# An eight-head masked attention layer: the work in front of the first attention row, reordered

## What is computed

```python
h = jnp.maximum(_layernorm(x, axis=-1), 0.0)
q = (h @ Wq + bq).reshape(b, n, H, HD)
k = (h @ Wk + bk).reshape(b, n, H, HD)
v = (h @ Wv + bv).reshape(b, n, H, HD)
scores = jnp.einsum('bqhd,bkhd->bhqk', q, k) / jnp.sqrt(jnp.float32(HD))
scores = scores + (1.0 - adj)[None, None, :, :] * -1000000000.0
attn = jax.nn.softmax(scores, axis=-1)
out = jnp.einsum('bhqk,bkhd->bqhd', attn, v).reshape(b, n, d)
return x + (out @ Wo + bo)
```

## Time and profile before

| | us |
|---|---|
| median of 3 runs | 1139.5 (1138.93 to 1139.97) |
| profiled execution, its own time | 1138.54 |
| span of the profiled execution | 1136.6 |
| PE busy | 1101.3 (97%) |
| ACT busy | 1019.7 (90%) |
| DVE busy | 964.0 (85%) |
| POOL busy | 131.5 (12%) |

### The profile page before, as it was taken

One profiled execution on the slowest core, in us unless ns is written; L12 is line 12 of the kernel. 1 busy time (PEld: TensorE's weight loads), 2 busy tenths in 40 slices (PEclk: granted clock), 3 DMA queues, 4 the chain that ended last, 5 costly groups with the idle time before them and its releaser, 6 DMA issues.

```text
span 1136.6 us, 28159 instructions
## 1 busy us (share of the span) xinstructions
PE 1101.3 (97%) x10756; PEld 894.8 (79%) x10756; DVE 964.0 (85%) x1747; ACT 1019.7 (90%) x1883; POOL 131.5 (12%) x234
## 2 busy tenths in 40 slices
PE   5599999999999999999999999999999999999997
PEld 4378888888878878888887878878887887878775
DVE  4599889988899888998889978898889988888875
ACT  2499999999999999999999999999999999999995
POOL 3102000021000210021001200012000021000001
PEclk9699999999999999999999999999999999999999
DMA  8532242423423243332423324242242323223101
GB/s 276 154 94 58 60 125 64 106 59 79 127 62 94 55 120 93 76 93 56 124 75 86 94 57 129 60 105 73 71 124 59 103 57 97 72 73 90 45 20 38
DMA packets 76596, 99.51 MB, mean 88 GB/s; under 512 B 17968, under 2 KB 43696, under 8 KB 76464
## 3 DMA queue, kind: packets, MB, share of 16 engines
q1 hardware_dynamic: 75504, 95.10, 31.6%
q0 software_dynamic: 576, 1.57, 0.6%
q10 hardware_dynamic: 384, 1.05, 0.3%
...
## 4 chain that ended last, share of the span: by engine, by line
PE 90%; ACT 6%; DVE 1%; ACTq 1%; issue 1%; DMA 1%; POOL 0%; DVEq 0%
PE ps_turn L693 29%; PE ps_scores L679 22%; PE ps_heads L756 18%; PE ps_side L700 9%; PE ps_side L727 5%; PE ps_side L709 5%; ACT rows L439 3%; ACT turned_a L444 1%; ACTq L278 1%; PE ps_turn L700 1%; PE ps_heads L716 1%; PE ps_heads L742 1%; ACT turned_b L449 0%; DMA xn<-in_x 0%; DVE rows L529 0%
## 5 line engine op out<-in xcount | busy, mean ns | idle before, releaser
L529 DVE CUSTOM_DVE_ANT_0 rows<-ps_scores,mask 128x1024 f32<-128x1024 f32 x512 | 613.0, 1215 | 32.0 <-issue 23.7
L439 ACT ACTIVATE rows<-rows,row_min 128x1024 f32<-128x1024 f32 x512 | 587.2, 1150 | 17.7 <-DVE row_min L529 17.4
L693 PE MATMUL ps_turn<-ident_r,rows_raw 128*128 128x128 f32 x4096 | 462.9, 256 | 6.6 <-ACT turned_a L444 4.9
L693 PEld LDWEIGHTS ps_turn<-ident_r,rows_raw 128*128 128x128 f32 x4096 | 399.0, 141 | 74.0 <-issue 35.5
L444 ACT ACTIVATE turned_a<-ps_turn 128x512 f32<-128x512 f32 x512 | 305.5, 597 | 52.1 <-PE ps_turn L693 52.0
L679 PE MATMUL ps_scores<-k_stack,q_stack 128*128 128x512 f32 x1024 | 317.5, 422 | 12.8 <-DMA k_stack<-start_k_lo 12.1
L536 DVE COPY turned_b<-ps_turn 128x512 f32<-128x512 f32 x328 | 225.6, 688 | 35.8 <-PE ps_turn L693 27.1
L679 PEld LDWEIGHTS ps_scores<-k_stack,q_stack 128*128 128x128 f32 x1024 | 167.1, 189 | 35.8 <-issue 14.8
L417 POOL COPY inv_wide<-row_inv 128x256 f32<-128x256 f32 x64 | 25.5, 399 | 943.9 <-DVE row_inv L564 916.1
L756 PE MATMUL ps_heads<-turned_a,v 128*32 128x256 f32 x2048 | 123.8, 382 | 0.6 <-ACT inv_wide L474 0.6
L756 PE MATMUL ps_heads<-turned_b,v 128*32 128x256 f32 x2048 | 122.2, 379 | 0.0
...
## 6 DMA issues: line engine op xcount, KB each, us to landing
q_stack<-q_hi SPq DMA_DIRECT2D x240, 64.0 KB, 2.0
q_stack<-q_lo SPq DMA_DIRECT2D x240, 64.0 KB, 2.0
k_stack<-k_hi SPq DMA_DIRECT2D x240, 64.0 KB, 2.0
k_stack<-k_lo SPq DMA_DIRECT2D x240, 64.0 KB, 2.0
...
```

What stands on the lines that cost most here:

```text
L439: nc.scalar.activation(rows[:, k, :], rows[:, k, :], ACT.Exp, bias=row_min[:, k:k + 1], scale=-1.0, accum_out=row_sum[:, u % 2, j:j + 1]). ...
L529: nc.vector.tensor_tensor_reduce(out=rows[:, k, :], in0=ps_scores[n % 2][:], in1=mask[:, qt, :], scale=1.0, scalar=START_MIN, op0=ALU.add, ...
L693: tr = nc.tensor.transpose(ps_turn[half][:, k, :].bitcast(F32R), rows_raw[:, n % RING, kt * P:(kt + 1) * P], ident_r[:])
```

## The change

- PE runs 20 matmuls of the identity (128x512, WARM) before its first real work.
- START_STEPS is reordered: q's first half, k's first half, then the second "ht" pair, k's second half, q's second half. Counts that followed s now follow the place in START_QK. The start tiles are 512 wide; the second halves use the steady tiles `q_hi`, `k_hi`, `q_lo`, `k_lo`.
- The stack copies of the start are made by halves, in DMAs of 64 KB: q's first half (16) by POOL; k's first half (16) by SP; k's second half by ACT for heads 0 and 1 (8), by POOL for head 2 (4), by SP for head 3 (4). q's second half (16) is issued by SP after the fourth row's scores. So 48 DMAs of 64 KB (3 MB) stand ahead of row 3, where 32 of 128 KB (4 MB) stood.
- x of batch 0 is loaded in three pieces; the first two hold two tiles each.
- Mask tile 1 is loaded early and converted by DVE between the low parts. Tiles 2 and 3 and tiles 4 to 7 are loaded by SP after the fourth row's scores and converted by POOL, tile by tile (`late_masks`). The load of x for batch 1 and the first two of the residual stand behind them.
- In batch 0 no moments of batch 1 are taken before row 8; those of tiles 0 to 3 all follow row 8.
- ACT's high part of q for phase 1 now waits for all 16 copies of q's second half out of `q_hi` (`stack_count` gives 4 DMAs per head for it, 1 before).

```diff
-START_STEPS = (("ht", 0), ("ht", 1), ("qk", 0), ("ht", 2), ("ht", 3), ("qk", 1), ("qk", 2), ("qk", 3),
+START_STEPS = (("ht", 0), ("ht", 1), ("qk", 0), ("qk", 1), ("ht", 2), ("ht", 3), ("qk", 3), ("qk", 2),
                ("v", 0), ("v", 1))
+START_QK = [s for kind, s in START_STEPS if kind == "qk"]
+WARM = 20
+MASKS_EARLY, MASKS_LATE = 2, 4
...
             count = (fills * CHUNKS + steps_more) * STEP_DMAS
             if g == 0:
-                first = PARTS - POOL_COPIES if n == "q" else 0 if h < ACT_HEADS else PARTS
-                count += first - CHUNKS * STEP_DMAS
+                count -= STEP_DMAS if n == "q" else CHUNKS * STEP_DMAS
...
+            sp.wait_ge(lo_done, START_QK.index(1) + 1)
+            stack_step(sp, 0, 1, start_stacked, high=start_hi, low=start_lo)
+            sp.wait_ge(lo_done, START_QK.index(3) + 1)
+            stack_step(sp, 0, 3, start_stacked, range(ACT_HEADS + 1, PARTS))
+
+            sp.wait_ge(scores_done, PARTS)
+            load_mask(2, MASKS_EARLY, MASKS_LATE)
+            stack_step(sp, 0, 2, stacked["q"][0])
+            load_mask(3, MASKS_LATE, TILES)
+            load_x(1)
             load_res(0, 0)
             load_res(0, 1)
...
-            pool.wait_ge(lo_done, QK_STEPS - 1)
-            for h in range(PARTS):
-                stack_start(pool, pool_stacked[h], h, "q", range(POOL_COPIES))
+            pool.wait_ge(lo_done, START_QK.index(0) + 1)
+            stack_step(pool, 0, 0, pool_stacked, high=start_hi, low=start_lo)
+            pool.wait_ge(lo_done, START_QK.index(3) + 1)
+            stack_step(pool, 0, 3, pool_stacked, range(ACT_HEADS, ACT_HEADS + 1))
...
+            def late_masks(part, first, end):
+                pool.wait_ge(mask_in[part], 16)
+                for t in range(first, end):
+                    pool.tensor_scalar(mask[:, t, :], mask[:, t, :], 1.0, -MASKED, ALU.subtract, ALU.mult
+                                       ).then_inc(mask_ready, 1)
+
+            late_masks(2, MASKS_EARLY, MASKS_LATE)
...
-            act.wait_ge(lo_done, QK_STEPS)
-            for h in range(ACT_HEADS):
-                stack_start(act, act_stacked[h], h, "k", range(PARTS))
+            act.wait_ge(lo_done, START_QK.index(3) + 1)
+            stack_step(act, 0, 3, start_stacked, range(ACT_HEADS))
...
-            for s in range(QK_STEPS):
-                cols = slice(s // 2 * BANK, (s // 2 + 1) * BANK)
-                low_part(0, 0, s, start_lo[s % 2][:, cols], start_hi[s % 2][:, cols], QK_BANKS[s % 2])
+            for k, s in enumerate(START_QK):
+                low_part(k + 1, 0, s, (start_lo + lo)[s][:], (start_hi + hi)[s][:], QK_BANKS[k % 2])
...
-                    if g == 0 and STATS[t] == i and not last:
+                    if g == 0 and i == max(STATS[t], 0 if b else UNIT_ROWS) and not last:
                         moments(b + 1, t)
...
+            for _ in range(WARM):
+                nc.tensor.matmul(ps_scores[1][:, 0:BANK].rearrange("p (k n) -> p k n", n=P), ident_r[:],
+                                 ident_r[:].unsqueeze(1).to_broadcast([P, PARTS, P]), start=True, stop=True)
```

105 lines of the change are left out of this document (53 added, 52 removed).

## The result

The changed kernel takes 1133.33 us (median of 5 runs, 1132.61 to 1133.84) where the kernel before takes 1139.48 (5 runs, 1138.93 to 1139.97): a ratio of 0.9946, with a 95% interval from 0.9932 to 0.9961. The medians are 6.15 us apart, the two profiled executions 5.05 (1138.54 and 1133.49; spans 1136.6 and 1131.3).

A forecast was written before the change was run, and what follows sets the result against it. The prediction took PE as the bound, reached through the copies of the start, the first turn and ACT. Its terms, -9.9 + 2.3 + 1.2 = -6.4 us, took the median from 1139.5 to 1133 us, range 1129.5 to 1136.5.

The forecast's parts named there:

- Term one: Start of the kernel: earlier low parts and half-size copies bring the first turn 9.9 us sooner; bounds -11.5 and -6.6.
- The ceiling of 245 GB/s: Copies of the start: the most the DMA engines were taken to move, about 245 GB/s.
- the split over three queues: Copies of the start: POOL and SP issue alone until 23.1 us, then ACT joins and each issue stretches to 0.80 us.
- The stall of 3.83 us: POOL's copy issue: the 3.83 us stall should go away with DVE's large mask instruction, by contention with VectorE.
- Term two: Phase 1: ACT's high part of q waits for SP's 16 copies out of `q_hi`, losing 2.3 us, from 1.2 to 4.
- The rival in which the wait costs nothing: ACT's wait before `q_hi` costs nothing and the moments hide too: 1130 us, chance 0.20.
- Term three: Batch 1's four moments on DVE ahead of mask row 13 lose 1.2 us, from 0 to 1.3.
- At no cost: Batch 1's x, late mask tiles, residual and SP's phase 1 copies come in time; a POOL mask tile takes 2.2 us at most.
- the slower rival: x of batch 1 lands late for DVE's slot 8, after 59 us, making the kernel slower: 1142 us, chance 0.04.
- The sum: Whole kernel: -9.9 + 2.3 + 1.2 = -6.4 us, giving a median of 1133 us.

The follow-up runs named there:

- e6_fill: e5_both plus 14 identity matmuls before row 0's scores and 5 before row 1's, to keep PE busy: 1132.98 us, ratio 0.9946.
- e1_cold: Changed kernel without its 20 identity matmuls at the start (WARM = 0): 1135.35 us, ratio 0.9966.
- e3_stats: Changed kernel with batch 1's moments of tiles 0 to 3 after rows 10, 12, 13 and 15 instead of all after row 8: 1133.68 us, ratio 0.9953.
- e5_both: Changed kernel with the edits of e2_qbuf and e3_stats together: 1132.26 us, ratio 0.9935.
- e7_pool_prices: Changed kernel with POOL converting the late mask tiles by different instruction forms, same values: 1131.18 us, one run.
- e2_qbuf: Changed kernel with q's second half of the start in a buffer of its own, so ACT's high part need not wait for its copies: 1132.51 us, ratio 0.9945.
- e4_masks_early: Changed kernel with the late mask tiles loaded ahead of the copies instead of after the fourth row's scores: 1134.94 us, ratio 0.9962.
- e12_after_fills: Changed kernel with identity matmuls 22, 4 and 4 at the start, 14 and 5 before rows 0 and 1, without e2_qbuf's or e3_stats's edit: 1133.52 us, ratio 0.9953.
- e11_before_fills: Kernel before the change with added identity matmuls only: 22 and 4 at the start, 36 and 14 before rows 0 and 1: 1135.44 us, ratio 0.9973.
- e9_balance: e6_fill with more identity matmuls at the start, and one head's k copies moved from ACT to POOL: 1127.91 us, ratio 0.9908.

## Why the prediction came out right

The forecast of 1133 and the measured 1133.33 are nearer together than the terms are to theirs. The path was the one forecast: copies, first turn, ACT's wait for `q_hi`, the moments, PE. The sizes were off both ways.

**Term one, -9.9: measured -9.24.** DVE's first moments came 1.38 us sooner than before (0.6 forecast), the low parts 0.4 to 1.0 sooner than forecast, row 0 at 29.64 (29), row 1 at 31.70 (31.8). The ceiling of 245 GB/s held in this execution (the mean of the three stretches of the earlier trace rows is 258, and others reached 267), and so did the split over three queues. What was mis-sized is behind row 1: the sum let its mask end at 33.8, but row 3 started at 34.41, because PE had idled for 4 us before row 0 and the clock fell to 0.50 at 30.9 (the forecast had PE busy until 27.5 and idle for 1.5; its last work ended at 25.65); e6_fill puts the price of the half-speed rows at 1.03 us up to the first turn. The clock was low there in the kernel before too (0.60 and 0.50 in the earlier trace rows), so it takes nothing from the difference between the two, only from what was promised. Two details of the start were off in opposite senses. DVE wasn't fed from the first piece on: it waited 1.18 us for the third, and all eight moments stand before the normalization. And the matmuls of the identity took 7.28 us, not up to 10. That they warm PE is shown by e1_cold; what this is worth at the first turn is 1.2 there and more in e3_stats and e5_both. And -9.24 is one pair of executions: with the same start up to row 3 and a warm PE, the first turn is 9.07 sooner than before in e7_pool_prices and 8.18 in e2_qbuf, and with a cold start 7.65 and 6.90 in e3_stats and e5_both. After's profiled start was one of the early ones.

POOL's issues took 0.50 us each but for the first and the third; SP and ACT at the same time:

```profile
24.26 0.98 POOL L288 DMA_DIRECT2D k_stack<-k_hi  x2
25.24 0.98 POOL L288 DMA_DIRECT2D k_stack<-k_lo  x2
26.80 1.65 ACTq L288 DMA_DIRECT2D k_stack<-k_lo  x2
30.68 1.22 SPq L288 DMA_DIRECT2D k_stack<-k_lo  x2
```

The stall of 3.83 us is gone with DVE's large mask instruction, and the DMA engines are 0.92 full here all the same. The third issue shows a small stall of the same kind, while the DMA engines are only 0.55 full (17 to 18 us):

```profile
17.15 0.68 DVE L625 TENSOR_SCALAR mask<-mask 128x1024 f32<-128x1024 f32 x1
17.19 0.74 POOL L288 DMA_DIRECT2D q_stack<-start_q_hi  x1
```

It ends 0.10 us after DVE's conversion of mask tile 1, as the long one ended 0.10 after the large conversion (32.06 and 31.96); in e5_both, too, the issue beside tile 1 takes 0.81 and ends 0.10 after it. That is what the Trainium skill, GPSIMD Engine Reference, section Key points, would have: contention with VectorE, not a full queue. In which mode DVE was, no run here shows. ACT's issues took 0.70 to 1.02 against the 0.80 assumed and began at 21.33, 1.8 sooner, and SP's last copy was issued by 31.9 against 31.7.

**Term two, +2.3: measured +1.78.** The mechanism is the one forecast, ACT idle for 1.57 us, released by a copy into `q_stack`, near 45 to 47.5 (47.67). The working of when the wait ends was good to 0.2: 45.2 plus 2.3 is 47.5. But the other side of the race, when ACT would get there, was set 0.9 too early (45.2, where ACT was free at 46.10), 0.66 of it from term one. Of the 1.78 us, e2_qbuf gives 1.18 back at once; behind it stood 0.64 of PE's half speed. The rival in which the wait costs nothing is out.

**Term three, +1.2: measured +0.9 where PE takes over, +1.3 by unit 3**: from `k_lo` (-7.46) to the point where PE takes over (-6.56). The order was as forecast: mask rows 11 and 12, four moments, mask row 13, ACT idle for 0.92. From `q_hi` to unit 3 e2_qbuf, whose clock did not fall there, takes 1.3 more than before. The reason given, that the four stand in one slot, holds for 0.2 of it only; the rest stays when they are spread.

**No term: the clock.** The idle time that the moments give PE was followed by 3.4 us at 1.2 GHz, which cost 0.9 by unit 3 (39.79 against e2_qbuf's 38.90 from `q_hi` on; 0.6 to 1.0 in the four executions with such a fall). Together: -9.24 + 1.78 + 1.29 + 0.89 = -5.28, the distance at unit 3. The rows that would have warned me are the earlier trace rows: behind the long idle time of PE in the trace of before the clock was at 0.50 to 0.60. With moments in slot 8 the clock fell between 64.7 and 69.6 in four executions of six (after, e4_masks_early, e7_pool_prices, e12_after_fills); with the moments spread it fell there in none of six.

**At no cost: held, with one price wrong.** x of batch 1 was there in time, DVE is not idle before its first moment at 58.41, so the slower rival is out. But a mask tile on POOL takes 3.7 us, not "2.2 at most":

```profile
41.52 7.39 POOL L431 TENSOR_SCALAR mask<-mask 128x1024 f32<-128x1024 f32 x2 [15.29 <-DMA mask<-in_adj]
54.45 14.76 POOL L431 TENSOR_SCALAR mask<-mask 128x1024 f32<-128x1024 f32 x4 [1.21 <-DMA mask<-in_adj]
```

Tiles 4 to 7 end at 69.2 instead of 64, and the next work of POOL starts at 70.94. The row that I priced from was an add followed by a multiply with scalars from tiles, another form of the same instruction. Had POOL's next work been 2 us sooner, this would have been on the path.

**The sum.** By the trace the gain is 5.3 us at unit 3, not 6.4: term one brought 0.66 less, the clock took 0.9 that no term had and the moments 0.1 more, while term two cost 0.5 less than forecast. The medians show 6.15, because the kernel before loses a further 1.1 to 1.4 us against the changed one over the rest of the span (2.2 against e7_pool_prices), in a part of the program that the diff doesn't touch. More than half of it comes in three steps near 345, 745 and 1060 us of before, 0.2 to 0.4 each. What makes them is not settled: they show against every changed kernel and not against e11_before_fills, which has the same early part as before. So the nearness of forecast and median is partly luck, and the range of 7 us was the honest size.

Not settled either: why the clock falls again after the first matmuls of the identity in some executions and not in others, and what e9_balance's split of the copies is worth by itself.
